# GpSimd drains ahead of every group of gathers in three layers of a four-layer graph network

## The reference

```python
h = jnp.maximum(_layernorm(x), 0.0)
# layer 0: sums of relation products, one of 16 matrices per edge
msg = sum_r (h[src] * (type16 == r)) @ W0[r];       out = segment_sum(msg, dst)
# layer 1: mean of the sources
agg = segment_sum(h[src], dst);  out = elu(agg / cnt @ Wl.T + bl + h @ Wr.T)
# layer 2: messages
m = silu(concat[h[src], h[dst], edge_attr] @ w1 + b1) @ w2 + b2; agg = segment_sum(m, dst)
# layer 3: attention over the edges of a destination, 4 rules, 8 relations
score = q[dst] . (h[src] @ Wk1 + rel_emb[type8] @ Wk2 + bk) + q[dst] . key_rule
out = segment_sum((h[src] @ W3[type8]) * mean_r softmax(score_r), dst)
```

## Time and profile before

| | us |
|---|---|
| median of 2 runs | 2630.01 (2622.27 to 2637.75) |
| span of the profiled execution | 2690.8 |
| POOL busy | 1543.2 (57%) |
| PE busy | 1523.2 (57%) |
| DVE busy | 1051.5 (39%) |
| ACT busy | 487.3 (18%) |

### The profile page before, as it was taken

The page is one execution under the profiler, slowest core; times in us unless marked ns, Lnnn a source line. Parts: engine busy times, 40 slices in busy tenths (PEclk is TensorE's granted clock), DMA queues, the critical chain, the costliest instruction groups (busy, mean ns, idle before and its releaser), DMA issues.

```text
span 2690.8 us, 27765 instructions
## 1 busy us (share of the span) xinstructions
PE 1523.2 (57%) x8443; PEld 1343.0 (50%) x8443; DVE 1051.5 (39%) x2213; ACT 487.3 (18%) x1153; POOL 1543.2 (57%) x1509
## 2 busy tenths in 40 slices
PE   5545332424478888765376667659553536445564
PEld 2224332424367777765376666658332325435554
DVE  4446110111556565633122222223524634334467
ACT  2100000000356666501000000001211111001020
POOL 5447766764667777735566666662344556665620
PEclk8656555555677777766555655657656766666677
DMA  6432122120111111103122222222341212222210
GB/s 199 130 110 86 24 84 58 36 61 16 30 31 36 34 37 34 33 12 65 37 52 50 57 51 51 58 51 44 110 162 52 65 54 66 61 55 68 58 39 13
DMA packets 159861, 159.26 MB, mean 59 GB/s; under 512 B 108361, under 2 KB 111993, under 8 KB 158748
## 3 DMA queue, kind: packets, MB, share of 16 engines
q1 hardware_dynamic: 111372, 89.07, 11.7%
q0 software_dynamic: 48352, 68.42, 11.5%
HBM read 118.71 MB, written 46.06 MB: 61 GB/s over the span
## 4 chain that ended last, share of the span: by engine, by line
another core or an unknown queue 30%; DVE 21%; PE 17%; issue 16%; POOL 10%; DVEq 2%; ACT 1%; DMA 1%; SPq 1%; ACTq 0%; POOLq 0%
POOL flat L583 10%; DVE flat L824 7%; PE ps L1353 4%; DVE oh L785 2%; DVE oh L1043 2%; PE ps L1388 2%; PE ps L1511 2%; DVE msg L1034 2%; DVEq L333 1%; PE ps L1341 1%; DVE msg L960 1%; DVE ohT L791 1%; PE ps L1325 1%; PE ps L1509 1%
## 5 line engine op out<-in xcount | busy, mean ns | idle before, releaser
L583 POOL DMA_INDIRECT flat<-table,flat x1061 | 1122.8, 1058 | 639.7 <-issue 314.7
L1388 PE MATMUL ps<-flat,oh 128*128 x1664 | 328.9, 380 | 368.1 <-DVE oh L785 255.3
L785 DVE TENSOR_TENSOR oh<-iota_n,drel 128x1024 f32<-128x1024 f32 x156 | 190.1, 1223 | 867.8 <-remote 605.0
L1388 PEld LDWEIGHTS ps<-flat,oh 128*128 128x128 f32 x1664 | 314.3, 291 | 394.7 <-issue 392.7
L583 POOL DMA_INDIRECT flat<-table,tile_idx x359 | 346.7, 966 | 267.9 <-DVE base L1037 140.2
L1353 PE MATMUL ps<-msg,oh 128*128 128x64 f32 x832 | 173.3, 393 | 156.5 <-ACT msg L1209 135.4
L1353 PEld LDWEIGHTS ps<-msg,oh 128*128 128x128 f32 x832 | 166.6, 304 | 160.4 <-issue 160.4
L1366 PE MATMUL ps<-uvT,flat 128*128 128x192 bf16 x2200 | 229.3, 275 | 25.7 <-ACT flat L1191 17.2
L1366 PEld LDWEIGHTS ps<-uvT,flat 128*128 128x128 bf16 x2200 | 219.8, 112 | 34.6 <-issue 29.3
L1576 PE MATMUL ps<-qn,ohT 128*128 x832 | 159.0, 349 | 124.9 <-issue 104.0
L1511 PEld LDWEIGHTS ps<-uvT,ohT 128*128 128x128 f32 x832 | 178.3, 291 | 64.3 <-issue 48.9
(11 more groups left out here) (320 smaller groups left out, 1481.9 us busy)
## 6 DMA issues: line engine op xcount, KB each, us to landing
table<-flat SPq DMA_DIRECT2D x52, 512.0 KB
drow<-slot_node SPq DMA_DIRECT2D x104, 256.0 KB
flat<-table,flat POOLq DMA_INDIRECT x1061
flat<-edge_attr_by_slot SPq DMA_DIRECT2D x52, 128.0 KB
edge_attr_padded<-edge_attr SPq DMA_DIRECT2D x1, 6250.0 KB
flat<-table,tile_idx POOLq DMA_INDIRECT x359
flat<-tile_source SPq DMA_DIRECT2D x22, 256.0 KB
edge_attr_by_slot<-flat SPq DMA_DIRECT2D x2, 2048.0 KB
```

The source lines that it names most:

```text
L583: nc.gpsimd.indirect_dma_start(dest(t % PLACES), None, table, at_).then_inc(tile_gat[k % TRING], 16)
L785: V.tensor_tensor(oh[:, b], iota_n[:].unsqueeze(1).broadcast_to([P, SG, P]), drel[:, g * SG:(g + 1) * SG].unsqueeze(2).broadcast_to([P, SG ...
L1388: last = T.matmul(acc[:, bass.ds(n[j] * pitch + shift, width)], oh[:, b % 2, j, :], got[:, bass.ds(place[j], width)], start=False, stop=Tr ...
```

## The change

A function `breath()` is added on GpSimd, which is one `drain` instruction: GpSimd's sequencer goes on when all of its older instructions are complete. It is called ahead of each tile group's gathers, from the second group on, in the first layer, the message layer and the attention, behind the group's semaphore waits. That is 3 times 48, 144 drains. The mean layer, the gathers ahead, the edge attributes and all other engines' programs stay as they are. The order of the other instructions is the same on every engine; only their line numbers shift (L583 becomes L586, L594 becomes L599).

```diff
+            def breath():
+                pool.drain()
+
             for g in range(TG):
                 if g >= TRING:
                     pool.wait_ge(s("used"), g - TRING + 3 + 3)
+                if g:
+                    breath()
                 gather_tiles(0, g, table0_d.rearrange("n (r d) -> (n r) d", d=D), lambda p: got0[:, p, 0:D], tile_idx0)
...
             for g in range(TG):
                 if g >= TRING:
                     pool.wait_ge(s("edge_sum"), g - TRING + 3 + 2)
+                if g:
+                    breath()
                 gather_tiles(2, g, table2_d[:, :], lambda p: got0[:, p, 0:D], tile_idx1)
...
                     pool.wait_ge(s("scored"), k - TRING + 3 + 3)
                     pool.wait_ge(s("values"), k - TRING + 3 + 1)
+                if k:
+                    breath()
                 gather_tiles(3, k, table3_d.rearrange("n (r d) -> (n r) d", d=2 * D), lambda p: got3[:, p, :], tile_idx3)
```

## The result

| | before | changed |
|---|---|---|
| median of 2 runs, us | 2630.0 (2622.3 to 2637.8) | 2692.9 (2687.0 to 2698.8) |
| ratio | | 1.022, 95% interval 1.015 to 1.028 |
| span of the profiled execution, us | 2690.8 | 2685.2 |
| POOL busy / PE busy, us | 1543.2 / 1523.2 | 1535.4 / 1594.7 |

The change made the kernel 2.2% slower (1.5 to 2.8%); 2575 was forecast, 2% faster. The two profiled executions, however, are equally long. That gap between the timed and the profiled comparison is the first thing that the experiments had to explain.

The account below looks back on a forecast made before the run. GpSimd's back-to-back gathers were taken to hold up TensorE's signals. Layer sums of +25, -9 and -89 gave -73, so the profiled 2690.8 became 2618; scaled towards the timed runs, 2575 us was forecast, range 2490 to 2690.

Parts of the forecast that it names:

- What bounds the kernel, and who frees whom: While GpSimd runs gather after gather, TensorE's signals come late, and come through when GpSimd rests; 30% of the chain.
- The rival in which the stall is not GpSimd's doing: TensorE's late signals have another cause, so drains free little: sum +173, about 2800 us; 0.14, including freed only in part.
- The drain waits for the landing: A drain on GpSimd holds until the group's gathers have landed their data, not only until their descriptors are written.
- 1.71 + 0.25 = 1.95 us: Gap ahead of each group: landing plus restart instead of 0.30, 1.65 us more; 79 us per layer, 237 in all.
- The rival of the short drain: A drain ends when descriptors are written, in 0 to 0.3 us, stalls stay: 2630 to 2673 us; chance 0.16.
- The edge attributes: First layer: holds after its four edge attribute gathers, taken as 2 MB each, last 5.6 us instead of 1.95, adding 14.
- What the rest sets free: Readers keep up and GpSimd's waits go; with the drains' cost first layer +25, message layer -9, attention -89.
- the last groups of the first layer: At the first layer's end four slot groups are left instead of five after the last gather: -10 us.
- the step to the attention: After the message layer's last gather four slot groups are left instead of eight: up to -20 us, -14 taken.
- the +22 for longer gathers: Message layer: gathers that start inside a VectorE one-hot take longer, 0.45 us a group, +22 us.
- The reference: Timed runs are 2.3% shorter than the profiled execution; scaling 2618 by that gives 2559, and 2575 was taken.
- less than four fifths of the gain: Turning point: 356 us gained against 283 paid; if less than four fifths of the gain comes, the change costs time.

Follow-up runs that it names:

- busy: The kernel before, with two iotas on GpSimd (1.49 us rest, no wait for a landing) where the change has each drain; with stalls 2555 us against 2631, 0.972.
- older_b: The kernel before, with a wait for the landing four groups back instead of each drain, so no rest; with stalls 2635 us against 2631, 0.999.
- landed: The kernel before, with GpSimd waiting for the previous group's landing instead of each drain; without stalls 2591 us against 2229, 1.163.
- before_again: The kernel before once more, unchanged, for a second trace; it met no stalls, 2229 us, and the kernel before beside it 2229.
- before_fourth: The kernel before, unchanged, traced beside its timed runs with stalls; 2704 us, span 2702.4.

## Why the prediction was wrong

**What bounds the kernel, and who frees whom: right, for its condition.** Engines waited for TensorE while GpSimd gathered, and went on when it rested. That a rest frees them, and not a signal that they share with GpSimd, is shown by `busy` against `older_b`: the pause waits for no other engine. The rival in which the stall is not GpSimd's doing is out for the three layers. What the trace of one execution could not tell is that the stalls are a condition: some 470 of its 2690 us, of which 69 + 106 + 132 = 307 lie in the three layers (546, 608 and 590 us against 477, 501 and 458).

The Trainium skill's rule that PE and ACT never wait on anyone (page "SBUF — State Buffer", section "Who interferes with whom") is about the ports of SBUF. Without stalls the trace agrees: no engine has a "remote" wait. With stalls a pause of GpSimd decides how long ScalarE waits for a signal: 64.9 us at most in `older_b`, 10.4 in `busy`. Whether the operation or only the delivery of its signal is late is not told by these traces.

**The drain waits for the landing: right. Its length: the first step that failed.** "So the gap ahead of a group would be about 1.71 + 0.25 = 1.95 us" took the landing from a matmul's start in the profile. It measured 2.57 us. The 1.71 was about right for a reader: in `landed` TensorE's first row starts 1.76 us after the gather's end (median), VectorE's copy and ScalarE's in the attention 1.62 and 1.71, and only VectorE's `msg` 2.31 (in the rows above 1483.83 - 1481.49 = 2.34). GpSimd itself goes on 2.26 us after that end, and a drain adds 0.3. The 0.25 for its restart was read behind a VectorE row; behind a landing it takes 0.7, and why is open. So each hold cost 2.25 more than the usual gap, not 1.65, 144 x 0.6 = 86 us in all. That alone exceeds the whole forecast gain of 73. The rival of the short drain was wrong: the drain does not end with the gather's own row in the profile.

**The edge attributes.** "I add 4 x (5.6 - 1.95) = 14": the 5.6 was no landing. The kernel before does not wait there for the edge attributes; by the earlier trace rows that gap ended with TensorE's `used`. The landing times, where recorded, are 8.2 to 10.7 us from the row's start (`before_again`), and the holds behind them were 8.1 to 10.6 us, and three others early in the first layer, while SyncE's transfers of the weights and of 6,250 KB of edge attributes were under way (the DMA engines 68% busy from 123 to 141 us, 10% from 141 to 240), were 4.4, 5.7 and 17.2. Those seven are 45 us above the usual 2.55 in the run without stalls, so the first layer's drains cost 153 us instead of 93.

**What the rest sets free: right in kind, layer by layer.** Between the two traces: the end -42 (forecast -41), the last groups of the first layer -10 (-10), the step to the attention -30 (-14), the start -8 (nothing was forecast; it has no drains). That the -10 was met is luck: `before_fourth`, without a drain and with stalls, also has four slot groups left at the first layer's end (a run of x64). The gathers' stretches: first +85 (+35), message +16 (+5), attention -12 (-48). They miss by 50, 11 and 36 us: 48 x 0.6 = 29 in each, in the first layer the edge attributes and the early holds on top, in the message layer less, since the +22 for longer gathers did not come (391.5 us busy against 396.3), and in the attention a few holds of 3 to 4 us besides. The sum is -6 instead of -73.

**The reference: the second step that failed.** "The two timed runs are 2.3% shorter than the profiled execution" was turned into a scale for everything, with the remark that the 60.8 us might all be stalls, in which case nothing is gained by them. It is the latter: `before_fourth` shows that a trace is as long as its timed runs (within 1%), and the level of 2690 differs from that of 2630 in its stalls. The gain that the trace showed was thus 61 us larger than the timed runs had to give. The changed kernel has no stalls left to vary in its three layers. Against the trace of the lower level it is 2685.2 - 2626.3 = 59 us longer, as in the timed runs (63); -6 on the first pair of traces and +63 on the timed runs are the same result at two levels of the kernel before.

The turning point that the prediction named was "less than four fifths of the gain". It was not the gain that fell short: 356 us were forecast, and about 390 came at the upper level of stalls, 335 at the lower. The price did it: 395 us with every effect in it, where 237 + 14 + 32 = 283 was forecast. The time fell 3 us outside the stated range of 2490 to 2690.

## What to carry to other kernels

Before a change that cures waits is costed, find out whether the waits are there in every execution: compare the span of the trace with the timed runs, and take a difference of a few per cent as a sign that the thing to be cured varies, not as a scale. A hold is to be measured on the engine that is held: three of the four readers went on 1.6 to 1.8 us after the gather's row, GpSimd itself 2.2 to 2.35 behind a wait and 2.55 behind a drain, and no row of the trace before shows that. And a full drain is a dear way to pause: under stalls a pause of 1.5 us that waits for no other engine and no landing gained 2.8% where the drain lost 2.2%. Without stalls the drain cost 17.6%, and the pause, by the estimate above, 8%.

## What was not expected of the hardware

- The same kernel on the same chip took 2230 us in one set of runs and 2631 in another; within a set the runs agree within about 2%. In the slower condition engines that depend on TensorE stand for up to 65 us while GpSimd issues gathers at 1.25 us each (in the earlier trace rows ScalarE began 48 us after the end of the row that it waited for), and the profile lacks the landing times of the gathers. The start and the mean layer are longer too (in the table above 90 to 99 us against 70, and 486 to 491 against 451 to 455). What brings the condition about stays open; no run here controls it.
- A drain behind gathers of 128 rows holds GpSimd 2.55 us from the end of the last one, a wait for the last landing 2.25, a second drain right behind the first 0.05 to 0.1 more. The Trainium skill, page "DMA: Bandwidth & Descriptors", section "Anatomy of one DMA — SWDGE (gpsimd) path", gives about 2.0 us of fixed cost, most of it the confirmation that the data has arrived, and adds the bytes at 436 GB/s. By its formula a gather of 2 MB (2,097,152 bytes) takes an estimated 6.8 us. The trace is above both: 2.5 us from issue to landing for a small gather, and 8.7 and 8.8 us for the two gathers of 2 MB (`before_again`).
- A drain behind an ordinary gather took 17 us while other queues moved much (the gap before the gather at 140.24 of the changed kernel, the DMA engines 68% busy).
